# A graph network on one core: the product behind the node choice taken over a gathered list of the chosen rows, zero blocks stored ahead, and a small copy moved from VectorE to ScalarE

## What is computed

```python
def _sage_mean(x, src, dst, w_self, w_neigh, b):
    msg = x[src]
    summed = jax.ops.segment_sum(msg, dst, num_segments=n)
    deg = jax.ops.segment_sum(jnp.ones((src.shape[0],), x.dtype), dst, num_segments=n)
    mean = summed / jnp.maximum(deg, 1.0)[:, None]
    return x @ w_self + mean @ w_neigh + b
k = max(1, n // COMP_RATIO)                      # 1562 of 6250 nodes
h = jax.nn.relu(_sage_mean(x, src, dst, ws1, wn1, b1))
h = _sage_mean(h, src, dst, ws2, wn2, b2)
score = jax.nn.sigmoid(h @ w_score + b_score)[:, 0]
_, idx = jax.lax.top_k(score, k)
new_val = jnp.zeros((n, h.shape[1]), h.dtype).at[idx].set(h[idx])
d = jax.nn.relu(_sage_mean(new_val, src, dst, wu1, wnu1, bu1))
d = _sage_mean(d, src, dst, wu2, wnu2, bu2)
```

## Time and profile before

| | |
|---|---|
| median of 3 runs | 8647.3 us (8641.81 to 8652.49) |
| the profiled execution | 8667.18 us, span 8665.4 us |
| mean granted TensorE clock | 0.892 |
| stage e | from about 6874 to 8665 us of the span |
| the choice, without matmuls of L2463 | from about 7737 to 7799 us |

### The profile page before, as it was taken

How to read it: one execution, slowest core, us unless ns; L and a number is a source line. 1 busy time by engine, 2 the same in 40 slices (tenths; PEclk the granted TensorE clock), 3 DMA queues, 4 the chain that set the end, 5 groups by cost and what they waited for, 6 DMA issues and landing times. The chain is left out here.

```text
span 8665.4 us, 151826 instructions
## 1 busy us (share of the span) xinstructions
PE 6356.4 (73%) x40296; PEld 4385.5 (51%) x40297; DVE 4445.3 (51%) x11924; ACT 2214.7 (26%) x4744; POOL 3409.5 (39%) x3460
## 2 busy tenths in 40 slices
PE   0366612666666579999976777767778599979999
PEld 0255501444444336555546777756667455545555
DVE  6877754666767522222227777767777601121111
ACT  1221201443444310100004555535555200000000
POOL 0777776656566100000007777647777200000000
PEclk6688856888999889999989999989998799989999
DMA  0122201322223346776752222222222266646666
GB/s 16 42 71 69 72 6 38 98 93 86 94 94 98 58 142 172 185 189 164 186 135 55 54 54 54 52 51 54 55 54 54 64 190 191 188 140 188 192 191 181
DMA packets 871731, 903.11 MB, mean 104 GB/s; under 512 B 421539, under 2 KB 820226, under 8 KB 864867
## 3 DMA queue, kind: packets, MB, share of 16 engines
q1 hardware_dynamic: 753541, 637.16, 26.8%
q0 software_dynamic: 109664, 179.92, 9.7%
q10 hardware_dynamic: 8064, 80.29, 2.3%
HBM read 722.84 MB, written 93.87 MB: 94 GB/s over the span
## 5 line engine op out<-in xcount | busy, mean ns | idle before, releaser
L1920 POOL DMA_INDIRECT d_row_ring<-table_att,src_at x1664 | 1583.3, 952 | 657.6 <-issue 489.9
L2463 PE MATMUL psum<-e_a_ring,e_parts 128*128 128x448 bf16 x8232 | 1578.7, 353 | 83.0 <-DVE e_parts L2545 76.4
L2463 PEld LDWEIGHTS psum<-e_a_ring,e_parts 128*128 128x128 bf16 x8232 | 806.5, 98 | 824.4 <-issue 88.4
L777 POOL DMA_INDIRECT b_row_ring<-edge_attr,b_entry x896 | 897.9, 1002 | 593.1 <-SPq L754 352.9
L796 PE MATMUL psum<-b_hot 128*128 x2920 | 666.9, 368 | 612.9 <-DVE b_hot L978 476.0
L354 POOL DMA_INDIRECT listed<-a_record,a_slot_no x832 | 868.4, 1044 | 316.1 <-issue 273.5
L1328 PE MATMUL psum<-c_a_ring,c_parts 128*128 128x448 bf16 x4116 | 816.3, 357 | 48.6 <-DMA c_a_ring<-adjacency 44.0
L1945 PE MATMUL psum<-edges_out,edges_in 128*128 128x120 f32 x4896 | 710.5, 306 | 158.4 <-ACT edges_in L2011 157.6
L796 PEld LDWEIGHTS psum<-b_hot 128*128 x2920 | 289.2, 99 | 964.4 <-issue 840.7
L1945 PEld LDWEIGHTS psum<-edges_out,edges_in 128*128 128x128 f32 x4896 | 658.9, 216 | 203.7 <-issue 203.7
L978 DVE TENSOR_SCALAR b_hot<-b_iota,b_key_dst 128x896 int16 (+1 forms) x1460 | 690.8, 473 | 4.6 <-issue 4.2
(11 more groups left out here) (433 smaller groups left out, 7895.4 us busy)
## 6 DMA issues: line engine op xcount, KB each, us to landing
e_a_ring<-adjacency SPq DMA_DIRECT2D x1372, 224.0 KB, 2.8
c_a_ring<-adjacency SPq DMA_DIRECT2D x686, 224.0 KB, 2.9
adjacency<-b_line ACTq DMA_DIRECT2D x49, 1568.0 KB
a_cum<-edge_attr SPq DMA_DIRECT2D x103, 512.0 KB
d_row_ring<-table_att,src_at POOLq DMA_INDIRECT x1664
b_row_ring<-edge_attr,b_entry POOLq DMA_INDIRECT x896
listed<-a_record,a_slot_no POOLq DMA_INDIRECT x832
e_a_left<-adjacency_left SPq DMA_DIRECT2D x28, 224.0 KB, 3.2
```

The costliest lines, as they stand in the source:

```text
L777: pool.indirect_dma_start(out=row_ring[:, u % 4, g, 0:D], out_offset=None, in_=a["edge_attr_128"], in_offset=bass.IndirectOffsetOnAxis(ap= ...
L1920: pool.indirect_dma_start(out=row_ring[:, u % 4, g, :], out_offset=None, in_=table_att[layer], in_offset=bass.IndirectOffsetOnAxis(ap=src_ ...
L2463: mm = nc.tensor.matmul(psum[:, 2 * (turn % 2) + v, 0:WIN], parts[:, piece, s, :], a_ring[:, s % SEVEN, v * WIN:(v + 1) * WIN], start=(s = ...
```

## The change

Three edits. **Stage b:** ScalarE stores zeros to all seven windows of the last tile row of `adjacency_left` ahead of the stage's main loop, and when no count is large only the last window is computed afterwards, not seven.

**Stage d:** the write-back of the peak is taken from VectorE's `peak` and put behind the exponent in ScalarE's `shrink`; VectorE waits for it before it reads the accumulated peak in the next visit.

**Stage e:** `choose` goes on: a count and a running sum give each chosen node a place in a list of 13 x 128 (FT = 13), two 0/1 tables (`in_tile`, 6272 elements to a partition, and `told`, three times 637) are multiplied in 49 small matmuls, and this yields the list of node numbers. During d = 1 SyncE stores `Y` to `table_few` (`keep`). GpSimd gathers the 13 groups of listed rows from it, `split_few` makes their parts, and the passes of d = 2 have 13 blocks, whose rows of `adjacency` GpSimd gathers by the list (91 indirect DMAs of 128 pieces of 1792 bytes), where SyncE loaded 49. `H` and its parts are still made, for the own-row product and for the block of `adjacency_left`.

```diff
+                for w in range(NWIDE):
+                    act.dma_start(adjacency_left[NT - 1, :, w * WIDE:(w + 1) * WIDE], blank[:]).then_inc(s_left_out, 16)
...
-                for k, (few, many) in enumerate(((1, NT), (NWIDE, NWIDE), (1, NW // 2))):
+                for k, (few, many) in enumerate(((1, NT), (1, NWIDE), (1, NW // 2))):
...
-                    act.wait_ge(s_scale, at + 1)
+                    act.wait_ge(s_scale, at + 2)
...
-                def shrink(at, h):
+                def shrink(at, h, code):
                     act.wait_ge(s_drop, at + 1)
-                    nc.scalar.activation(scale[:, h, :], drop[:, h, :], ACT.Exp).then_inc(s_scale, 1)
+                    nc.scalar.activation(scale[:, h, :], drop[:, h, :], ACT.Exp)
+                    nc.scalar.copy(acc[:, bass.ds(code[0], 1), FEAT:].rearrange("p a f -> p (a f)"), peaks_cut[:]
+                                   ).then_inc(s_scale, 1)
...
+                    dve.wait_ge(s_scale, at + 1)
...
-                    B.by(V.tensor_copy(now, peaks_cut[:]))
...
+            in_tile = a_ring[:].rearrange("p s f -> p (s f)").rearrange("p (t f) -> p t f", f=P)
+            told = parts[:].rearrange("p k t f -> p (k t f)")[:, 0:NT * 3 * FT].rearrange("p (t k q) -> p t k q", k=3, q=FT)
...
+            BLOCKS = [FT if d == 2 else NT for d, _ in PASSES]
+            FIRST = [sum(BLOCKS[:i]) for i in range(len(BLOCKS))]
...
+                def keep(p):
+                    sp.wait_ge(s_tile, 2 * (SEVEN + p + 1))
+                    t0 = p * SEVEN
+                    sp.dma_start(table_few[t0 * P:(t0 + SEVEN) * P, :].rearrange("(t p) f -> p t f", p=P),
+                                 Y[:, t0:t0 + SEVEN, :]).then_inc(s_load, 16)
+
                 for turn, (d, p) in enumerate(PASSES):
-                    for s in range(NT):
-                        n, slot = turn * NT + s, s % SEVEN
...
-                    for s in range(NT):
+                    for s in range(NT if d != 2 else 0):
...
+                    if d == 1 and p >= 2:
+                        keep(p - 2)
+                    if (d, p) == (1, SEVEN - 1):
+                        keep(SEVEN - 2)
+                        keep(SEVEN - 1)
...
+                pool.wait_ge(s_load, 16 * (LOADS + SEVEN))
+                pool.wait_ge(s_count, CHOSEN + 1)
+                for q in range(FT):
+                    pool.indirect_dma_start(
+                        out=few[:, q, :], out_offset=None, in_=table_few,
+                        in_offset=bass.IndirectOffsetOnAxis(ap=listed_at[:, q:q + 1], axis=0)
+                        ).then_inc(s_few_ring, 16)
+                for turn, (d, p) in enumerate(PASSES):
+                    for q in range(FT if d == 2 else 0):
+                        n = FIRST[turn] + q
+                        pool.wait_ge(s_used, USED + n - SEVEN + 1)
+                        pool.indirect_dma_start(
+                            out=a_ring[:, n % SEVEN, :], out_offset=None, in_=pieces,
+                            in_offset=bass.IndirectOffsetOnAxis(ap=piece_at[:, p, q:q + 1], axis=0)
+                            ).then_inc(s_piece_ring[n % SEVEN], 16)
...
-                    for s in range(NT):
+                    over, both = (2, (5, 9)) if d == 2 else (4, (9, 17))
+                    for s in range(BLOCKS[turn]):
...
+                            pe.wait_ge(s_parts, (FEW_NO if d == 2 else part_no(d, 0)) + s // SEVEN + 1)
+                        if behind and s == over:
-                        if behind and s in (9, 17):
-                            multiply(turn - 1, (9, 17).index(s))
-                        pe.wait_ge(s_block[s % SEVEN], 16 * ((BEFORE + turn) * SEVEN + s // SEVEN + 1))
+                        if behind and s in both:
+                            multiply(turn - 1, both.index(s))
+                        if d == 2:
+                            m = p * FT + s
+                            hold(pe, s_piece_ring[m % SEVEN], ring0 + 16 * (m // SEVEN + 1), s_held_pe)
...
+                    if (d, p) == (2, 0):
+                        pe.wait_ge(s_parts, part_no(2, SEVEN))
...
+                        pe.wait_ge(s_count, 2 * SEARCH + 1)
+                        nc.tensor.matmul(psum[:, 7, 0:DIGITS], lower[:], hits[:], start=True, stop=True).then_inc(s_count, 1)
+                        pe.wait_ge(s_count, 2 * SEARCH + 3)
+                        for t in range(NT):
+                            mm = nc.tensor.matmul(psum[:, 7, 0:3 * FT], in_tile[:, t, :], told[:, t, :, :].rearrange("p k q -> p (k q)"),
+                                                  start=(t == 0), stop=(t == NT - 1))
+                        mm.then_inc(s_count, 1)
...
-                            act.wait_ge(s_used, USED + (turn + 1) * NT + (k + 1) * SEVEN)
+                            if d == 0:
+                                act.wait_ge(s_used, USED + FIRST[turn + 1] + (k + 1) * SEVEN)
...
+                        for k in range(2):
+                            split_few(k)
                         for k in range(SEVEN):
-                            act.wait_ge(s_count, 2 * SEARCH + k + 1)
                             split(2, k)
...
+                def split_few(k):
+                    n = min(SEVEN, FT - k * SEVEN)
+                    grp = slice(k * SEVEN, k * SEVEN + n)
+                    V.tensor_tensor(few[:, grp, :], few[:, grp, :], bc(listed_real[:, grp], 2, [P, n, D]), ALU.mult
+                                    ).then_inc(s_count, 1)
+                    dve.wait_ge(s_high, FEW_NO + k + 1)
+                    dve.wait_ge(s_parts, FEW_NO + k)
+                    V.tensor_tensor(rest[k % 2][:, 0:n, :], few[:, grp, :], few_parts[:, 0, grp, :], ALU.subtract
+                                    ).then_inc(s_rest, 1)
+                    dve.wait_ge(s_mid, FEW_NO + k + 1)
+                    V.tensor_tensor(few_parts[:, 2, grp, :], rest[k % 2][:, 0:n, :], few_parts[:, 1, grp, :], ALU.subtract
+                                    ).then_inc(s_parts, 1)
...
+                    st.by(V.tensor_reduce(hits[:, 0:1], chosen[:], AX_X, ALU.add))
+                    st.by(V.tensor_tensor_scan(place[:], ones[:, 0:NT], chosen[:], 0.0, ALU.mult, ALU.add))
+                    counted(SEARCH)
+                    st.by(V.scalar_tensor_tensor(place[:], place[:], psum[:, 7, 0:1], chosen[:], ALU.add, ALU.mult))
+                    st.settle(dve)
+                    st.by(V.tensor_scalar(place[:], place[:], -1.0, None, ALU.add))
+                    st.settle(dve)
+                    st.by(V.tensor_copy(place_int[:], place[:]))
+                    st.settle(dve)
+                    st.by(V.tensor_scalar(place_int[:], place_int[:], 7, None, ALU.logical_shift_right))
+                    st.settle(dve)
+                    st.by(V.tensor_copy(place_tile[:], place_int[:]))
+                    st.settle(dve)
+                    st.by(V.scalar_tensor_tensor(place[:], place_tile[:], -128.0, place[:], ALU.mult, ALU.add))
+                    st.by(V.tensor_tensor(told[:, :, 2, :], bc(place_tile[:], 2, [P, NT, FT]), bc(count_row[:, 0:FT], 1, [P, NT, FT]),
+                                          ALU.is_equal))
+                    st.settle(dve)
+                    st.by(V.tensor_tensor(in_tile, bc(place[:], 2, [P, NT, P]), bc(count_row[:], 1, [P, NT, P]), ALU.is_equal))
+                    for k in range(2):
+                        st.by(V.tensor_tensor(told[:, :, k, :], told[:, :, 2, :], bc(node_two[:, k, :], 2, [P, NT, FT]), ALU.mult))
+                    counted(SEARCH + 1)
+                    st.by(V.tensor_copy(listed_f[:], told_sum[:, 1, :]))
+                    st.by(V.tensor_copy(listed_real[:], told_sum[:, 2, :]))
+                    st.settle(dve)
+                    st.by(V.scalar_tensor_tensor(listed_f[:], told_sum[:, 0, :], 64.0, listed_f[:], ALU.mult, ALU.add))
+                    st.settle(dve)
+                    st.by(V.tensor_copy(listed_at[:], listed_f[:]))
+                    st.by(V.tensor_scalar(listed_7[:], listed_f[:], float(SEVEN), None, ALU.mult))
+                    st.settle(dve)
+                    st.by(V.tensor_tensor(piece_at[:], bc(listed_7[:], 1, [P, SEVEN, FT]), bc(count_row[:, 0:SEVEN], 2, [P, SEVEN, FT]),
+                                          ALU.add))
+                    st.settle(dve)
+                    dve.sem_inc(s_count, 1)
                     for k in range(SEVEN):
                         grp = slice(k * SEVEN, (k + 1) * SEVEN)
                         V.tensor_tensor(H[:, grp, :], Y[:, grp, :], bc(chosen[:, grp], 2, [P, SEVEN, D]), ALU.mult
                                         ).then_inc(s_count, 1)
+                    dve.wait_ge(s_count, CHOSEN + SEVEN + 1)
+                    hold(dve, s_few_ring, gathered(dve) + 16 * FT, s_held_dve)
+                    for k in range(2):
+                        split_few(k)
+                    for k in range(SEVEN):
                         split(2, k)
 
```

(13 more changed lines are left out.)

76 lines of the change are left out of this document (59 added, 17 removed).

## The result

The changed kernel takes 8351.3 us (median of 4 runs, 8345.5 to 8353.4), the kernel before in the same session 8647.2: the ratio is 0.9657, with a 95% interval of 0.9642 to 0.9672, 296 us less. The profiled execution took 8351.0 us, at its median, while that of before stood 20 us over its own. Between the two traces lie 316.3 us, and 20 of them are no part of the change.

What follows compares the result with a forecast made beforehand. No engine is busy throughout (TensorE 73%, VectorE 51%), so each stage has its own limit, TensorE alone in stage e. The terms sum to -301.3 us, taking the median from 8647.3 to 8346 us, range 8318 to 8392.

Steps and rivals of the forecast that it cites:

- Stage b: End of stage b: six of seven windows go, zero stores cost at worst 2.5 us; -61.5 us.
- Stage d: Attention loop: the peak copy leaves VectorE, 0.08 us for each of 306 visits, 24.5 us before losses; -20 us.
- Four fifths should come through: Stage d: the share of the 24.5 us kept, as GpSimd's waits are where VectorE's lag is; -20 us.
- The list: Stage e, making the list, its gathers and parts: TensorE starts 46.5 us behind instead of 5.4; +41.1 us.
- Pass 0: First pass of d = 2: 29.4 us with TensorE idle about 12, before 58.56; -29.2 us.
- Passes 1 to 6: Passes of d = 2: 36 blocks fewer each at 1.135 us, a pass then 19.8 us; -245.2 us.
- From d = 2 to d = 3: Transition in stage e: ScalarE's six splits delay evacuating pass 6, so TensorE waits; +11.5 us.
- Clock: Stage e, after each of two 12 us stalls: first blocks may run slower, 0 to 3.6 us; +2 us.
- The rival that slab gathers set the pace: Passes of d = 2: gathers at 2.25 us pace them, deciding from 1.52 us; 57 us more, 8403; 12 in 100.
- The rival that ends slower: Passes of d = 2: 91 slab gathers would have to take 449 us; 8647 us or more; 2 in 100.

Runs made afterwards that it cites:

- e1: Kernel before with the edit of stage b alone (zeros stored ahead, one window at the stage's end): 11254.0 against 11319.6 us, ratio 0.9942.
- e2c: Kernel before with the attention edit alone (peak copied on ScalarE), third session: 8630.3 against 8642.0 us, ratio 0.9984.
- e5: Changed kernel with VectorE's seven multiplies into H moved behind the list's gathers, between each split's two subtractions: 10970.3 us, ratio 0.9757.
- e3: Changed kernel with ScalarE evacuating the seventh pass of d = 2 behind the first split of the next parts, not behind six: 11006.2 us, ratio 0.9725.
- e10: Changed kernel with the attention edit undone, VectorE copying the peak again: 10946.7 us, ratio 0.9741.
- e8: Changed kernel with each of the 91 slab gathers followed by a second one into an unread spare buffer: 8431.1 us, ratio 0.9753.
- e4: Changed kernel with the left block of d = 2's first pass moved behind block 10 of the second, its evacuation, transposes and multiplies later too: ratio 0.9735.
- e2: Kernel before with the attention edit alone (peak copied on ScalarE), first session: ratio 1.0004.
- e2b: Kernel before with the attention edit alone (peak copied on ScalarE), second session: ratio 0.9992.

## Why the prediction was right

8346 us were predicted, 8351 measured, in a range of 8318 to 8392. The mechanism held in all three stages; term by term, predicted and measured:

- **Stage b**, -61.5: -60.4 in the trace, -60.8 in e1, in the mean -60.6. Five spacings of 10.25 and the last window's 11.7 were the right reading; the zero stores are hidden.
- **Stage d**, -20: -12 by the medians of e2c, with 7 to 22 open; -19 and -22 between single traces. The sign was right. GpSimd's waits were to fall by some 25 us, from 85.5 to about 60, and fell by 12 to 14, from 82.7 to 70.8 and 68.4, half as much, as the gain did. The copy on ScalarE is hidden as said: `widened` waits for VectorE's comparison 278 times, 365.8 us in all, where it waited 273 times, 422.8 us, before. "Four fifths should come through" was the generous step: of 24.5 us about half does. By the starts of L2130 and L2136, sorted by place in the loop's turn of three, a visit of the first layer went from 6.63, 7.46 and 6.84 us (medians) to 6.49, 7.43 and 6.82: in the first layer the gain sits mostly in one visit of three, not 0.08 us in each. With -12 the account closes: -60.6 - 12 + 36.5 - 272.9 + 14.5 = -294.5, measured -296.
- **The list**, +41.1: +36.5. The operations up to `H` took 14.65 us, not 18.7. The largest single error is the 49 matmuls, 1.85 us where 5.5 were put. The price was an eighth of the 0.62 us of the earlier trace rows, 78 ns. But those matmuls start 56 ns apart at a granted clock of 1.00, the 0.62 us hold the 0.22 of the last one, and they have 128 columns where these have 39. The 49 start 33 ns apart, at a granted clock of 0.50: the lower clock was rightly expected, and the columns were left out. Gathers with the slowing 18.5, not 19.35: beside `H` they came every 2.0 us, not every 2.25. In both rows one gather passes to two of VectorE's operations: here they start 1.00 us apart, and in stage b, beside the gathers of the earlier trace rows, 1.13. The slowing itself is shown by e5. The ends given for this term, 33 and 50, do not follow from their conditions: 2.25 us for every gather and 7.6 for the matmuls make about 53, no slowing and 3.8 about 36, just under what was measured. By the Trainium skill (SBUF — State Buffer, section "SBUF: two separate sides") the side that comes second fully blocks for the whole instruction; the trace agrees for one operation (6.45 us beside 5.88). What it does not bear out is the prediction's reading for a row of them, that no gather ends before the row does: gathers of 1.23, 1.70 and 1.69 us ended during the seven back-to-back operations.
- **Pass 0**, 29.4 us: 30.3, with an idle stretch of 10.65 where about 12 were said. A split each 3.29 us held to the hundredth.
- **Passes 1 to 6**, 19.8 us: 19.78. The rule that a block that goes takes 1.135 us with it held, since nothing else fills a pass: the gathers need 16.3 of its 19.8 us, VectorE is busy for 4.2 of 20. It gave -244.7 for -245.2; most of the difference is in the slow blocks behind the first stall.
- **From d = 2 to d = 3**, +11.5: 11.39 idle, at the place named, and by the cause named (e3).
- **Clock**, +2: 1.1 us on the left block, 0.5 behind it, 2.9 at the transition, 4.5 in all, over the bound of 3.6. The bound was twice the 1.8 us of one start, whose clock of 0.72 is the mean of 6 us. Read in two halves, that start too began at 0.50 (7799 to 7802 us in the trace of before) and was at 0.94 in the next 3 us; the restart at the left block is alike, 0.50 and 0.95. What the bound left out is that one start can last longer than another: at the transition the clock stayed at 0.50 for 6 us, and at the left block it did so for 5.5 us in e3 and e10, where that block and the two behind it took 2.8 and 2.9 us too long, not 1.6.

The rival that slab gathers set the pace is answered by the trace, e8 and e4: at 1.25 us they do not, the price of twice as many is 80 us, and in the one stretch where they take 1.65 they would, if TensorE were not waiting for the splits anyway. The rival that ends slower needed 4.9 us per slab; the longest took 1.8.

That the total came within 5 us of the measurement is partly luck: the list was put 4.6 us too dear, stage d 8 too generous, and the clock 2.5 too cheap.

## What to carry to other kernels

When an engine is the only one in a chain, work taken from it pays in full until the next engine's count of instructions is reached. That point is worked out from the pitch of its instructions (here 1.25 us a gather), not from bytes, and it moves when another engine crowds it (1.65 beside the splits). A shortened stage also uncovers what its length had covered: look up each handover that was ordered for the old length, here ScalarE's six splits ahead of an evacuation, which cost 13 to 14 us and are had back by exchanging a few lines.

And measure a gain of a few us by medians, since one profiled execution can stand 20 us off.

## What the runs showed of the hardware

Not expected: the same program ran at two speeds in different sessions, 8642 us and 11,236 to 11,320. It is no trait of one device, since the same one gave 11,320 in one session and 8642 in a later one. Stage d's gathers with the same kernel in two sessions (duration least, median, most; first and last start):

```profile
L1920 POOL DMA_INDIRECT d_row_ring<-table_att,src_at x1664: 938/944/5517, 5814.1 to 9374.1; - x185
```

```profile
L1920 POOL DMA_INDIRECT d_row_ring<-table_att,src_at x1664: 938/944/5523, 4520.5 to 6735.4; - x185
```

No gather is slower (median 944 ns in both), but the stage takes 3560 and not 2215 us. Time comes in between the instructions, and one place where it shows is the loop's own work: VectorE's register instructions behind L978 last at most 111 ns in the kernel before's trace and 728 in e2's,

```profile
L978 DVEq FUSED_REGOPS  x1460: 69/76/111, 1456.0 to 3060.7; - x183
```

```profile
L978 DVEq FUSED_REGOPS  x1460: 3/76/728, 2279.8 to 4379.8; - x183
```

though the median is 76 ns in both. Stage e, whose passes are unrolled, took 1776.3 us in e2b and 1776.9 in e2c, both with the old stage e. The Trainium skill (Runtime: NRT & Kernel Launch, section "Instruction fetch mechanics") says that a taken branch whose target is not in the current window forces a fetch before execution goes on. That fits slow loops beside a straight part of equal speed, but not yet that the same loops are fast in one session and slow in another; no run here tries it, so the cause stays open.
